# TensorE leaves out, by a table, the semaphore waits that its other waits already hold

## What is computed

```python
x = layernorm(x + L0_attn(x))         # causal attention, 16 heads, 32-wide rotary latents
x = layernorm(x + L0_xattn(ctx, x))   # linear attention, with a layer norm inside
x = layernorm(x + L0_ffn(x))          # FP4-quantised SwiGLU, 704 wide
x = layernorm(x + L1_attn(x))         # causal softmax part plus a second, unnormalised part
x = layernorm(x + L1_xattn(x, ctx))   # masked cross attention and a 1024-wide MLP
x = layernorm(x + L1_ffn(x))          # FP6-quantised linear layer
```

## Time and profile before

| | |
|---|---|
| three runs | 1011.55, 1012.51, 1013.29 us; median 1012.51 |
| the profiled execution | 1009.19 us, of which the span from first to last instruction is 1007.40 |
| mean granted TensorE clock | 0.941 of full speed |
| busy share | PE 85%, DVE 75%, ACT 65%, POOL 30% |
| instructions | 30,406 in all; PE 11,854 matmuls and as many weight loads |

### The profile page before, as it was taken

The page is one execution under the profiler, slowest core; times in us unless marked ns, Lnnn a source line. Parts: engine busy times, 40 slices in busy tenths (PEclk is TensorE's granted clock), DMA queues, the critical chain, the costliest instruction groups (busy, mean ns, idle before and its releaser), DMA issues.

```text
span 1007.4 us, 30406 instructions
## 1 busy us (share of the span) xinstructions
PE 855.5 (85%) x11854; PEld 678.3 (67%) x11854; DVE 751.0 (75%) x1885; ACT 656.1 (65%) x2539; POOL 302.0 (30%) x586
## 2 busy tenths in 40 slices
PE   5476778999999999989898989999998989887753
PEld 4354566777777777767676867777677768665642
DVE  7976585878787878878787879687878778575342
ACT  3324568595959595967778695959594867727341
POOL 0121212233333343333323323333333332222121
PEclk9778899999999999999999999999999999888876
DMA  9200300000000000000000000000000000000000
GB/s 325 106 6 1 96 1 26 1 16 7 26 7 26 8 22 6 11 22 18 16 18 15 8 26 7 26 7 26 7 24 4 17 11 7 10 6 7 7 7 5
DMA packets 24445, 24.92 MB, mean 25 GB/s; under 512 B 2304, under 2 KB 22640, under 8 KB 24176
## 3 DMA queue, kind: packets, MB, share of 16 engines
q1 hardware_dynamic: 24304, 22.98, 7.0%
HBM read 18.80 MB, written 2.10 MB: 21 GB/s over the span
## 4 chain that ended last, share of the span: by engine, by line
PE 54%; DVE 25%; ACT 10%; POOL 6%; issue 5%; DMA 1%; DVEq 0%; SPq 0%; POOLq 0%
PE bank L1197 27%; PE s_tile L1197 22%; DVE peak L977 5%; DVE rope_ L969 4%; ACT prob L711 4%; POOL rstd L578 3%; PE bank L1309 2%; ACT k_ L744 2%; DVE stats L928 2%; PE bank L1398 2%; DVE y_ L952 2%; DVE y_ L955 2%; POOL var_eps L576 1%; ACT x_ L759 1%; DVE cross_ L1030 1%
## 5 line engine op out<-in xcount | busy, mean ns | idle before, releaser
L711 ACT ACTIVATE prob<-s_tile,low 128x128 f32<-128x128 f32 x768 | 271.9, 401 | 15.3 <-DVE low L982 15.2
L711 ACT ACTIVATION_READ_ACCUMULATOR prob<-s_tile,low 128x1 f32 x768 | 185.4, 241 | 0.0
L977 DVE TENSOR_REDUCE peak<-s_tile 128x4 f32<-128x512 f32 x192 | 122.8, 681 | 26.4 <-PE s_tile L1197 26.4
L576 POOL TENSOR_TENSOR var_eps<-mean_var,rsq 128x1 f32<-128x1 f32 x144 | 31.2, 217 | 300.7 <-DVE mean_var L930 299.5
L650 ACT ACTIVATE probT<-bank 128x512 f32<-128x512 f32 x192 | 99.6, 616 | 10.3 <-PE bank L1398 9.6
L759 ACT ACTIVATE x_<-y_,shift,rstd 128x256 f32<-128x256 f32 x96 | 56.8, 606 | 62.6 <-POOL shift L584 62.4
L650 ACT ACTIVATE xt_<-bank 128x256 f32<-128x256 f32 x80 | 30.9, 386 | 98.8 <-PE bank L1309 98.0
L613 POOL TENSOR_TENSOR k_<-q_,q_scale 128x256 f32<-128x256 f32 x32 | 19.8, 617 | 216.2 <-DVE q_ L1078 216.2
L1398 PE MATMUL bank<-cst,prob 32*128 32x32 f32 x3072 | 62.5, 226 | 25.0 <-ACT prob L711 11.0
L578 POOL TENSOR_TENSOR rstd<-var_eps,rsq 128x1 f32<-128x1 f32 x144 | 80.2, 557 | 11.3
L1398 PEld LDWEIGHTS bank<-cst,prob 32*128 32x128 f32 x3072 | 55.3, 140 | 38.1 <-ACT prob L711 22.9
(11 more groups left out here) (191 smaller groups left out, 2008.3 us busy)
## 6 DMA issues: line engine op xcount, KB each, us to landing
xtin<-in_xT SPq DMA_DIRECT2D x16, 128.0 KB, 6.4
next_<-in_x SPq DMA_DIRECT2D x16, 128.0 KB, 7.1
ct_<-in_ctxT SPq DMA_DIRECT2D x16, 128.0 KB, 7.8
w<-in_w SPq DMA_DIRECT2D x2, 1024.0 KB, 10.0
out<-x_ SPq DMA_DIRECT2D x16, 128.0 KB, 1.7
next_<-x_ SPq DMA_DIRECT2D x16, 127.0 KB
rowt<-in_rows SPq DMA_DIRECT2D x1, 1664.0 KB, 8.8
w<-in_gate_up SPq DMA_DIRECT2D x2, 512.0 KB, 6.3
```

Source lines behind the costliest of these rows:

```text
L576: pool.tensor_tensor(var_eps[:, b:b + 1], mean_var[:, b, 1:2], rsq[:, 0:1], ALU.add) .then_inc(eps_in, 1)
L711: ins = act.activation(prob[:, r, c * P:(c + 1) * P], bank[r][:, c * P:(c + 1) * P], ACT.Exp, scale=SCALES[layer], bias=low[:, b, at0:at0 ...
L977: dve.tensor_reduce(peak[:, b, 4 * r:4 * r + 4], rows4(src[:, :]), AX_X, ALU.max)\
```

## The change

A table `COVERED` is added. Its key is a stage and the name of one of its waits (an operand such as `"x1_keys.k"`, a bank to be freed such as `"free.s1"`, or another such as `"pairs_done"`); its value is the range of tiles for which TensorE leaves this wait out, because others of its waits, here or earlier in its order, already hold it. The order of the stages, the banks, the operations and the waits of all other engines stay as they are. `need` and `need_empties` stand in front of `wait_ge` and `wait_empties`, and `free` asks the table too. The names under `l1_ma` in the table are `f1_turn_x.xt`, `free.s0`, `free.s1`, `free.s2`, `free.s3` (tiles 14 and 15 alone), `l0_lat.s0`, `l0_lat.s1`, `l0_lat.s2`, `l1_scores.s0`, `l1_scores.s1` and `pairs_done`; `l0_lat.s3` is not among them.

```diff
+COVERED = {
...
+    ("l0_mix0", "free.t3"): (2, 16), ("l0_mix0", "l0_scores.s2"): (1, 16), ("l0_mix0", "x1_turn_x.xt"): (0, 16),
...
+    ("l1_ma", "free.s0"): (0, 16), ("l1_ma", "free.s1"): (0, 16), ("l1_ma", "free.s2"): (0, 16),
+    ("l1_ma", "free.s3"): (14, 16), ("l1_ma", "l0_lat.s0"): (0, 16), ("l1_ma", "l0_lat.s1"): (0, 16),
+    ("l1_ma", "l0_lat.s2"): (0, 16), ("l1_ma", "l1_scores.s0"): (0, 16), ("l1_ma", "l1_scores.s1"): (0, 16),
+    ("l1_ma", "pairs_done"): (0, 16), ("l1_ma_value", "free.y"): (0, 16), ("l1_ma_value", "l1_ma.s0"): (0, 16),
...
+    ("x1_keys", "came_ctx"): (0, 16), ("x1_mix0", "free.t0"): (0, 16),
...
+    ("x1_scores", "free.s1"): (0, 16), ("x1_scores", "free.s3"): (0, 16),
...
+    ("x1_scores", "l1_ma.s1"): (0, 16), ("x1_scores", "l1_ma.s3"): (0, 16), ("x1_scores", "x1_keys.k"): (0, 16),
...
+}
...
+            def covered(stage, i, b, name):
+                first, last = COVERED.get((stage, name), (0, 0))
+                return i is not None and first <= i * GROUP + b < last
+
+            def need(stage, i, b, name, signal, value):
+                if not covered(stage, i, b, name):
+                    pe.wait_ge(signal, value)
+
+            def need_empties(stage, i, keys):
+                wait_empties(pe, i, [key for key in keys if not covered(stage, i, key[1], key[0] + "." + key[2])])
+
             def free(i, key, moved=()):
                 k, n = place(i, key)
-                wait_empties(pe, i, [m for m in moved if place(i, m)[0] != k])
+                need_empties(key[0], i, [m for m in moved if place(i, m)[0] != k])
                 if n > 0:
-                    pe.wait_ge(empty[k], n)
+                    if i is None or not covered(key[0], i, key[1], "free." + key[2]):
+                        pe.wait_ge(empty[k], n)
                     before_ = OCCUPANT[k, n - 1]
                     if before_[0] == "l0_lat" and k < 3:
                         last = WHERE["l0_lat", before_[1], "s3"]
-                        pe.wait_ge(empty[last[0]], last[1] + 1)
+                        if i is None or not covered(key[0], i, key[1], "l0_lat.s3"):
+                            pe.wait_ge(empty[last[0]], last[1] + 1)
                 return bank[k]
...
             def l1_ma(i, b):
-                pe.wait_ge(pairs_done, at("DVE", i, ["l1_project"], "l1_project", b))
+                need("l1_ma", i, b, "pairs_done", pairs_done, at("DVE", i, ["l1_project"], "l1_project", b))
```

More of the change, by code:

```diff
@@ L1312, in l0_project @@
             def l0_project(i, b):
-                pe.wait_ge(came_xT[b % 2], came_by(i, b // 2 + 1, 2))
+                need("l0_project", i, b, "came_xT", came_xT[b % 2], came_by(i, b // 2 + 1, 2))
                 xin = xtin[:, b % 2, :, :]
@@ L1318, in l0_v @@
             def l0_v(i, b):
-                pe.wait_ge(came_xT[b % 2], came_by(i, b // 2 + 1, 2))
+                need("l0_v", i, b, "came_xT", came_xT[b % 2], came_by(i, b // 2 + 1, 2))
                 dst = free(i, ("l0_v", b, "v"))
@@ L1323, in l0_lat @@
             def l0_lat(i, b):
-                wait_empty(pe, i, ("l0_project", b, "qk"))
+                need_empties("l0_lat", i, [("l0_project", b, "qk")])
                 for n in range(4):
@@ L1340, in l0_latent @@
                 key = ("l0_latent", b, "q")
-                pe.wait_ge(q_done, at("POOL", i, ["l0_rope"], "l0_rope", b))
+                need("l0_latent", i, b, "q_done", q_done, at("POOL", i, ["l0_rope"], "l0_rope", b))
                 dst = free(i, key)
@@ L1351, in f @@
                     if layer == "l0":
-                        pe.wait_ge(k_done, at("POOL", i, ["l0_rope"], "l0_rope", b))
-                        wait_empty(pe, i, ("l0_latent", b, "q"))
+                        need(stage, i, b, "k_done", k_done, at("POOL", i, ["l0_rope"], "l0_rope", b))
+                        need_empties(stage, i, [("l0_latent", b, "q")])
                     elif layer == "l1":
-                        wait_empty(pe, i, ("l1_project", b, "k"))
+                        need_empties(stage, i, [("l1_project", b, "k")])
                     else:
-                        wait_empties(pe, i, [("x1_project", b, "q"), ("x1_keys", b, "k")])
+                        need_empties(stage, i, [("x1_project", b, "q"), ("x1_keys", b, "k")])
                     for r in range(4):
@@ L1389, in f @@
                     keys, r = [(layer + "_mix0", b, f"t{g}") for g in range(4)], BANK_ORDER[n]
-                    wait_empty(pe, i, (layer + "_scores", b, S_BANKS[r]))
+                    need_empties(f"{layer}_mix{n}", i, [(layer + "_scores", b, S_BANKS[r])])
                     if n == 0:
@@ L1425, in f @@
                     dst = free(i, key)
-                    pe.wait_ge(inverse, at("DVE", i, INVERSES, layer + "_inv", b, 2, 1))
+                    need(layer + "_spread", i, b, "inverse", inverse, at("DVE", i, INVERSES, layer + "_inv", b, 2, 1))
                     for c in range(2):
@@ L1436, in f @@
                     if layer == "l1":
-                        pe.wait_ge(v_copied, at("ACT", i, ["l1_turn_x"], "l1_turn_x", b))
+                        need("l1_value", i, b, "v_copied", v_copied, at("ACT", i, ["l1_turn_x"], "l1_turn_x", b))
                     else:
@@ L1463, in turn_x @@
             def turn_x(i, stage, norm, b):
-                pe.wait_ge(x_new, at("ACT", i, NEW_X, norm, b))
+                need(stage, i, b, "normed", x_new, at("ACT", i, NEW_X, norm, b))
                 turn_tile(i, (stage, b, "xt"), x_[:, b, :])
@@ L1469, in x0_kv @@
                     pe.wait_ge(came["x0_w"], 16)
-                pe.wait_ge(came_ctx[b], came_by(i, 1, 1))
+                need("x0_kv", i, b, "came_ctx", came_ctx[b], came_by(i, 1, 1))
                 dst = free(i, ("x0_kv", b, "kv"))
@@ L1495, in f @@
                 def f(i, b):
-                    pe.wait_ge(dequant, at("POOL", i, QUANTS, quantized, b))
+                    need(stage, i, b, "dequant", dequant, at("POOL", i, QUANTS, quantized, b))
                     turn_tile(i, (stage, b, "xt"), xqu(b))
@@ L1503, in f0_up @@
                         wait_empty(pe, None, key)
-                wait_empty(pe, i, ("f0_turn_x", b, "xt"))
+                need_empties("f0_up", i, [("f0_turn_x", b, "xt")])
                 for j in range(2):
@@ L1510, in f0_up2 @@
             def f0_up2(i, b):
-                wait_empty(pe, i, ("f0_turn_x", b, "xt"))
+                need_empties("f0_up2", i, [("f0_turn_x", b, "xt")])
                 for j in range(2, 4):
@@ L1517, in f0_turn_h @@
             def f0_turn_h(i, b):
-                pe.wait_ge(dequant, at("POOL", i, QUANTS, "h_level", b))
+                need("f0_turn_h", i, b, "dequant", dequant, at("POOL", i, QUANTS, "h_level", b))
                 turn_tile(i, ("f0_turn_h", b, "t0"), hid(b), 4)
             def f0_turn_h2(i, b):
-                pe.wait_ge(dequant, at("POOL", i, QUANTS, "h_level", b))
+                need("f0_turn_h2", i, b, "dequant", dequant, at("POOL", i, QUANTS, "h_level", b))
                 key = ("f0_turn_h2", b, "t1")
@@ L1537, in f0_down2 @@
                 key = ("f0_down", b, "o")
-                wait_empty(pe, i, ("f0_turn_h2", b, "t1"))
+                need_empties("f0_down2", i, [("f0_turn_h2", b, "t1")])
                 filled(down(bank[place(i, key)[0]], b, range(4, FK)), i, key)
@@ L1565, in l1_ma_value @@
                 key = ("l1_ma_value", b, "y")
-                pe.wait_ge(e_done, at("DVE", i, ["l1_e"], "l1_e", b))
+                need("l1_ma_value", i, b, "e_done", e_done, at("DVE", i, ["l1_e"], "l1_e", b))
                 for r in range(4):
-                    wait_empty(pe, i, ("l1_ma", b, S_BANKS[r]))
+                    need_empties("l1_ma_value", i, [("l1_ma", b, S_BANKS[r])])
                 dst = free(i, key)
@@ L1574, in x1_keys @@
                     pe.wait_ge(came["x1_w"], 16)
-                pe.wait_ge(came_ctx[b], came_by(i, 1, 1))
+                need("x1_keys", i, b, "came_ctx", came_ctx[b], came_by(i, 1, 1))
                 dst = free(i, ("x1_keys", b, "k"))
@@ L1581, in x1_values @@
                     pe.wait_ge(came["x1_w"], 16)
-                pe.wait_ge(came_ctx[b], came_by(i, 1, 1))
+                need("x1_values", i, b, "came_ctx", came_ctx[b], came_by(i, 1, 1))
                 dst = free(i, ("x1_values", b, "v"))
@@ L1590, in x1_turn_h @@
             def x1_turn_h(i, b):
-                pe.wait_ge(affine, at("DVE", i, AFFINES, "x1_affine1", b, 2, 1))
+                need("x1_turn_h", i, b, "affine", affine, at("DVE", i, AFFINES, "x1_affine1", b, 2, 1))
                 turn_tile(i, ("x1_turn_h", b, "xt"), y_[:, b, :])
@@ L1613, in x1_down2 @@
                 key = ("x1_down", b, "o")
-                wait_empty(pe, i, ("x1_up2", b, "h1"))
+                need_empties("x1_down2", i, [("x1_up2", b, "h1")])
                 filled(down2(bank[place(i, key)[0]], b, range(4, 8)), i, key)
```

## The result

| | before | after |
|---|---|---|
| median of 20 runs each | 1012.76 us | 1001.89 us |
| ratio, with its 95% interval | | 0.9891 [0.9871, 0.9911] |
| the profiled execution | 1009.19 us | 1003.66 us |
| its span from first to last instruction | 1007.4 us | 1001.9 us |
| its mean granted clock | 0.941 | 0.934 |

What follows compares the result with a forecast made beforehand. The chain of work, 54% on TensorE, was taken as the bound, with waits costing only where TensorE runs dry. 3.0 + 0.9 + 0.5 + 0.5 = 4.9, say 5.0 us, off 1012.5 gave 1007.5; range 1002.0 to 1011.5.

Steps and rivals of the forecast that it cites:

- The price of a semaphore instruction: In TensorE's queue, each semaphore instruction after the one released costs 0.107 us where TensorE has run dry.
- `l1_ma`, 3.0 us: Before `l1_ma`, eight waits become four and two semaphore instructions go: 0.214 us, 14 times on the chain, 3.0 us.
- `x1_scores` and `x1_keys`, 0.9 and 0.5: On the chain, `x1_scores` saves 0.06 us 15 times, 0.9 us; `x1_keys` a usable 0.05 us 10 times, 0.5 us.
- The tile: Time between two `l1_ma` in the middle of the run: 53.15 to 53.3 us instead of 53.5.
- The count: EVENT_SEMAPHOREs in TensorE's queue in the changed kernel's profile: 243 instead of 978.
- Covered waits at nothing: Removed waits that run while TensorE still works on other stages, as at `l0_mix0`, save nothing.
- The off-chain places at nothing: `l1_mix0`, `l1_value` and `l0_lat`: 0.37 us a tile, 5 us together, taken at nothing because VectorE is still busy.
- Rival 1: Everything exposed counts, off-chain places too: 10.4 us gained in all, so 1002.1 us; chance 0.16.
- 1012.5 - 5.0 = 1007.5 for the median: Final step: the summed 5.0 us is taken off the median of the runs, giving 1007.5 us.
- rival 4: Slower by the clock: new low-clock stretches on TensorE, 1.2 us each, six or more giving 1014.7 us; chance 0.06.
- Rival 2: Covered after all, by an equal path or the queue: 0 to 2 us, about 1011.8; chance with rival 3 0.18.
- the rule on the queue: TensorE's queue of 64 lets the sequencer's waits lie ahead of the array, worth nothing: 1012.5 us.

Runs made afterwards that it cites:

- e3_lat: Changed kernel with `l0_lat.s3` added to the table, so `l1_ma` has one wait in tiles 0 to 13; 997.1 us, 0.9854 of the kernel before.
- f2_l1ma: Changed kernel with the table kept for `l1_ma` alone; 1005.8 us, 0.9943 of the kernel before.
- e2_rest: Changed kernel with the table lacking `l1_ma`, `x1_scores` and `x1_keys`; 1007.7 us, 0.9982 of the kernel before.
- e1_chain3: Changed kernel with the table cut to `l1_ma`, `x1_scores` and `x1_keys`; 1001.3 us, 0.9907 of the kernel before.
- f1_double: Kernel before with eight more equal bank 3 waits in each `l1_ma`, eight semaphore instructions instead of four; 1015.1 us, ratio 1.0035.
- f4_best: e3_lat plus `x1_scores`' doubled bank 0 wait left out and `l1_scores` asking for bank 3 first; 989.6 us, 0.9779 of the kernel before.
- g2_best: f4_best run again unchanged; 989.6 us, 0.9793 of the kernel before.
- g1_few: f4_best with the table cut to `l1_ma`, `x1_scores` and `x1_keys`; 996.5 us, 0.9871 of the kernel before.
- h2_best_shift: f4_best with 32 more satisfied waits at the first `l1_ma` only; 989.2 us, 0.9791 of the kernel before.
- h3_few_shift: g1_few with 32 more satisfied waits at the first `l1_ma` only; 997.1 us, 0.9853 of the kernel before.
- i2_minus: f4_best with `l1_mix0`, `l1_value` and `l0_lat` taken out of the table; 988.8 us, 0.9799 of the kernel before.
- h1_before_shift: Kernel before with 32 more satisfied waits at the first `l1_ma` only; 1013.6 us, ratio 1.0029.
- g4_shift: Changed kernel with 32 more satisfied waits at the first `l1_ma` only; 1004.9 us, 0.9970 of the kernel before.

## Why the prediction was wrong, and where it was right

- *The price of a semaphore instruction* was right: forecast 0.107 us each, measured 0.105 by adding four and (0.46 - 0.25) / 2 = 0.105 by leaving out two. The second one that was left (`e3_lat`) went too: 0.25 became 0.04.
- *`l1_ma`, 3.0 us*: right, 0.21 of a tile (`f2_l1ma`), at the places and with the waits that were named. The missing name `l0_lat.s3` was worth as much again.
- *`x1_scores` and `x1_keys`, 0.9 and 0.5*: right in sum, 0.30 - 0.21 = 0.09 of a tile, but not one by one. For `x1_scores` I had expected 0.14 after `q_`, so 0.06 saved; it is 0.09, so 0.11 saved, one semaphore instruction at its full price. The 0.14 comes from places where the semaphore instruction starts after the release; here it stood waiting already, 473 ns long. That alone makes the whole 0.09, which leaves next to nothing for `x1_keys`, although its own wait fell from 0.14 to 0.04; no run separates the two.
- *The tile*: 53.19, forecast 53.15 to 53.3. Times 16 it makes 16 x 0.30 = 4.8 us against a sum of 5.0. *The count*: 243, as forecast.
- *Covered waits at nothing*: right for a tile at full clock (`e2_rest`: 53.52). For the whole time it left out the gaps without a wait, see below.
- *The off-chain places at nothing*: right for the tile. The idle time before `l1_value` and `l1_mix0` fell by 0.16 and 0.21, and the table without them (`e1_chain3`) has the same tile as the whole one. Rival 1 gave the right number, 1002.1 us, by the wrong mechanism; the tile was not under 52.9, and nothing of the tile came from its places.
- *The step that failed* is "1012.5 - 5.0 = 1007.5 for the median": the sum of the waits was taken for the whole difference between two medians, with everything else the same in both, and it started from a median of three runs. The runs showed in its place a gain of 6.9 and 7.7 us in the repeats and 10.9 in the first comparison. 4.8 us of it are the tile's. The mean clock is worth 0 to 0.8 in the repeats (0.9404 against 0.9403, 0.9430 against 0.9414, at 5.2 us for 0.010). A gap of 1.0 us without a wait stands in the profile of before and in none of the changed kernel; how much of it reached the end is not shown. That leaves about 1 us, and each ratio is uncertain by 2 to 3.5. The other 3 to 4 us of the first comparison go with the kernel before, 1.7 to 4.2 us slower there than in the five others; the clocks of its runs there are not known, so the reason stays open. Only a loss by the clock was a rival (rival 4); a gain beside the chain was nowhere. That the measured 1001.9 lies only 0.1 us outside the range is the other side of this: a range that ended at rival 1 left no room for a chance gain.
- *Rival 2, and the rule on the queue* (the Trainium skill, Advanced Engine Details and Errata, Engine Queue Depths and Sequencer Loop): by it the sequencer's instructions would run ahead of the array and cost nothing. That holds where TensorE has work queued (`e2_rest`, 656 of them for nothing in the tile) and fails where it has run dry (`f1_double`, 0.105 us each). The trace had shown both.

Left open: all of why a kernel with 656 fewer covered semaphore instructions and the same tile is 7 us faster at the level of `f4_best` (6.9 between `g2_best` and `g1_few`, 7.9 between `h2_best_shift` and `h3_few_shift`). The two slower kernels have 3.2 and 3.5 us of gaps in their profiles, `f4_best`, `g2_best`, `h2_best_shift` and `i2_minus` none; and read off at an equal mean clock the 24 runs of these four and the 12 of the two are 3.1 us apart, with a standard error of 0.7. The two figures fit, but a profile is one execution. The rest, 3 to 4 us, goes with a mean clock that is 0.008 lower; whether the instructions or the gaps cause that is not shown. Against a simple answer stands `e1_chain3`, which has 2.2 us of gaps and was no slower than the changed kernel, which has none.

## What to carry to other kernels

Count the semaphore instructions in front of the stages at which an engine has run dry, and price only these: each was worth 0.105 us here, 656 others nothing in a tile at full clock. Look besides for gaps in which the engine waited for nothing that the profile shows: here, behind the first tile, they came only in the kernels with 788 such instructions or more. Of the waits that stay, let the one that ends last be the first in the source, where it rides on the instruction itself (0.04 instead of 0.14 us, as in `l1_scores`). And where the mean granted clock differs from run to run, take the time between two like points at full clock for the effect of an edit, and put the scatter of the clock into the range on both sides: a sum of path terms forecasts the tile, and the median may move by as much again.

## What the runs showed of the hardware

- A satisfied semaphore instruction in TensorE's queue shows as 51 ns but takes 0.105 us in a row of them (`f1_double`), and 1.8 us for 16 more in a row (32 waits, `h1_before_shift`). One that stands waiting already when it is released delays the next matmul by 0.09 to 0.10 us (`x1_scores` after) instead of 0.14 (`x1_keys` before).
- TensorE stood still for 0.9 to 1.3 us without a wait, one to three times, in each of the nine profiles with 788 to 1042 semaphore instructions in its queue, and in none of the eleven with 215 to 322, all behind 130 us.
- The clock of the last part differs from one profiled run to another: 0.81 instead of 0.74 was worth 4.6 us of 70.4. A stretch of low clock in the middle of the run lasts 3.4 us and costs 1.2 us (a tile of 54.4 against 53.2).
- 1.8 us of waits once, in the first tile, went with 4.0 us in the changed kernel (`g4_shift`) and with nothing in the best version (`h2_best_shift`); each figure is uncertain by 2 to 3.5 us.
